# A recommendation tower on one core: warm-up transposes, single-table rounds first, and gathers tied to the pair products

## The reference, cut to what matters

```python
e = jnp.stack([tbl_0[ids[:, 0]], ..., tbl_25[ids[:, 25]]], axis=1)      # (512, 26, 128)
all_vecs = jnp.concatenate([dense[:, None, :], e], axis=1)              # (512, 27, 128)
interactions = jnp.einsum('bnd,bmd->bnm', all_vecs, all_vecs)
z = jnp.concatenate([dense, interactions[:, rows, cols]], axis=1)       # rows < cols
h = jnp.concatenate([z, dense], axis=1)
h = jnp.maximum(h @ W_top1 + b_top1, 0.0)                               # 607 -> 512
h = jnp.maximum(h @ W_top2 + b_top2, 0.0)                               # 512 -> 256
y = h @ W_top3                                                          # 256 -> 1
```

## Time and profile before

| | |
|---|---|
| median of 3 runs | 140.96 us (140.27 to 141.63) |
| the profiled execution: its own time | 141.28 us |
| the profiled execution: span from first to last instruction | 139.5 us |
| mean granted clock of TensorE, share of full | 0.902 |
| PE, PEld busy | 108.0 us (77%), 83.7 us (60%) |
| DVE, ACT, POOL busy | 82.8 us (59%), 51.2 us (37%), 70.7 us (51%) |
| moved from memory | 16.27 MB |

### The profile page before, as it was taken

How to read it: one execution, slowest core, us unless ns; L and a number is a source line. 1 busy time by engine, 2 the same in 40 slices (tenths; PEclk the granted TensorE clock), 3 DMA queues, 4 the chain that set the end, 5 groups by cost and what they waited for, 6 DMA issues and landing times.

```text
span 139.5 us, 3355 instructions
## 1 busy us (share of the span) xinstructions
PE 108.0 (77%) x1416; PEld 83.7 (60%) x1416; DVE 82.8 (59%) x173; ACT 51.2 (37%) x86; POOL 70.7 (51%) x60
## 2 busy tenths in 40 slices
PE   0079299999999999989985422279999995995971
PEld 0057188778888888867743311267588684683560
DVE  5286396999999999979989100055035266014101
ACT  3040561794949678089160000012042131040130
POOL 4787788888888888888888777200000000000000
PEclk9999959999999999999997555555799999999999
DMA  2999999999999999981111112100000000000000
GB/s 65 236 281 239 303 237 262 234 244 240 239 247 236 285 275 220 230 260 50 38 38 42 51 44 56 38 7 5 0 5 5 5 5 0 0 5 5 0 0 3
DMA packets 7677, 16.49 MB, mean 118 GB/s; under 512 B 2007, under 2 KB 2648, under 8 KB 7662
## 3 DMA queue, kind: packets, MB, share of 16 engines
q1 hardware_dynamic: 5998, 12.87, 37.6%
q0 software_dynamic: 1664, 3.41, 9.9%
HBM read 16.27 MB, written 0.00 MB: 117 GB/s over the span
## 4 chain that ended last, share of the span: by engine, by line
PE 40%; DVE 23%; issue 16%; DMA 12%; ACT 4%; SPq 1%; another core or an unknown queue 1%; POOL 0%; DVEq 0%; POOLq 0%
DVE hot L422 14%; DMA tab_raw<-in_tbl 12%; PE gram_ps L543 12%; DVE tab_lo L426 6%; PE fill_ps L595 6%; PE l_ps L566 4%; PE fill_ps L507 3%; PE fill_ps L509 3%; ACT vec L233 2%; PE l_ps L569 2%; PE l_ps L573 2%; PE fill_ps L529 2%; PE l_ps L570 2%; PE turn_ps L581 2%; DVE vec L412 2%
## 5 line engine op out<-in xcount | busy, mean ns | idle before, releaser
L327 POOL DMA_INDIRECT gathered<-in_tbl,ids_sb x52 | 69.8, 1343 | 16.6 <-issue 14.9
L507 PE MATMUL fill_ps<-hot,tab_hi 125*128 125x512 f32 x112 | 47.1, 420 | 8.8 <-issue 8.3
L509 PE MATMUL fill_ps<-hot,tab_lo 125*128 125x512 f32 x112 | 45.9, 410 | 0.0
L422 DVE TENSOR_SCALAR hot<-ids_bc,row_id 125x1024 fp32r<-125x1024 int32 (+1 forms) x60 | 42.8, 714 | 3.3 <-DMA ids_bc<-in_ids_t 2.1
L507 PEld LDWEIGHTS fill_ps<-hot,tab_hi 125*128 125x128 f32 x112 | 22.6, 202 | 14.9 <-issue 9.0
L543 PE MATMUL gram_ps<-vec 128*32 128x27 f32 x1024 | 17.5, 208 | 13.8 <-issue 13.8
L344 ACT CAST tab_hi<-tab_raw 125x512 fp32r<-125x512 f32 (+1 forms) x30 | 17.9, 610 | 25.8 <-DMA tab_raw<-in_tbl 16.6
L426 DVE TENSOR_TENSOR tab_lo<-tab_raw,tab_hi 125x256 fp32r<-125x256 f32 (+1 forms) x60 | 24.0, 400 | 5.4 <-issue 4.4
L543 PEld LDWEIGHTS gram_ps<-vec 128*32 128x32 f32 x1024 | 14.3, 123 | 18.8 <-issue 18.8
L509 PEld LDWEIGHTS fill_ps<-hot,tab_lo 125*128 125x128 f32 x112 | 22.5, 201 | 4.4
L459 DVE COPY_PREDICATED pairs<-second,gram_ps 128x104 f32<-128x104 int32 x16 | 4.4, 274 | 31.3 <-ACT pairs L383 31.1
(11 more groups left out here) (46 smaller groups left out, 61.5 us busy)
## 6 DMA issues: line engine op xcount, KB each, us to landing
tab_raw<-in_tbl SPq DMA_DIRECT2D x8, 448.0 KB
ids_bc<-in_ids_t SPq DMA_DIRECT2D x13, 256.0 KB
tab_raw<-in_tbl SPq DMA_DIRECT2D x4, 560.0 KB
gathered<-in_tbl,ids_sb POOLq DMA_INDIRECT x52
w_raw<-in_w_pairs SPq DMA_DIRECT2D x3, 256.0 KB
w_sb<-in_W_top SPq DMA_DIRECT2D x1, 512.0 KB
tab_raw<-in_tbl SPq DMA_DIRECT2D x2, 224.0 KB
tab_raw<-in_tbl SPq DMA_DIRECT2D x8, 52.0 KB
```

The lines of the kernel that those rows point to most:

```text
L327: pool.indirect_dma_start(out=gathered[:, n % GSLOTS, j, :], out_offset=None, in_=tables[f], in_offset=bass.IndirectOffsetOnAxis(ap=ids_sb ...
L422: nc.vector.tensor_scalar(hot[0:HP, (PIECE * c + k) % HOTS, 0:n, :], ids_bc[0:HP, slot, 0:n, :], row_id[0:HP, j:j + 1], None, ALU.is_equal ...
L507: nc.tensor.matmul(into, tab_hi[0:HP, c % PSLOTS, f, k * D:(k + 1) * D], one_hot, start=first, stop=False)
L509: used = nc.tensor.matmul(into, tab_lo[0:HP, c % PSLOTS, f, k * D:(k + 1) * D], one_hot, start=False, stop=last)
```

## The change

- PE first does eleven transposes of the identity matrix into `turn_ps`, whose result nobody reads; its wait for the identity moves there from the dense step.
- The round of tables 3 and 6 is split, so that the first three rounds have one table each; there are eight rounds instead of seven. The order of the steps is rewritten: batches stand later by one or two places, and `batch(2, 2)` and `batch(2, 3)` come after the first units of tile 1.
- SP loads the dense vectors behind round 2; the first half of table 2 is loaded from ACT's queue instead of SP's.
- Nine of the last sixteen gathers wait for a count of `gram_made`, two for a count of `l1_made`. POOL works in order, so those behind them wait too.
- `fill_copy` of a batch walks the same elements in another order: the n vectors of a sample, which lie side by side in `vec`, are now the innermost loop.

```diff
-ROUNDS = [[2], [3, 6], [7, 8], [19, 21], [23, 25], [0, 4], [5, 12]]
-NK = [8, 8, 8, 8, 8, 10, 10]
+ROUNDS = [[2], [3], [6], [7, 8], [19, 21], [23, 25], [0, 4], [5, 12]]
+NK = [8, 8, 8, 8, 8, 8, 10, 10]
+WARM_UPS = 11
-    out = hot(0) + [("dense",)] + hot(1) + batch(0, 0) + batch(0, 1) + hot(2) + batch(0, 2) + batch(0, 3)
-    out += hot(3) + batch(1, 0) + batch(1, 1) + hot(4) + batch(1, 2) + hot(5) + batch(1, 3) + batch(2, 0)
-    out += hot(6) + batch(2, 1) + batch(2, 2) + gram(0, 0, 1, 2, 3)
-    out += gram(1, 0) + batch(2, 3) + [("turn", 0)] + gram(1, 1) + [("l1", 0)] + gram(1, 2) + [("h1t", 0)]
-    out += gram(1, 3) + [("l2", 0)] + gram(2, 0) + [("turn", 1)] + batch(3, 0) + gram(2, 1)
+    out = hot(0) + hot(1) + batch(0, 0) + hot(2) + [("dense",)] + batch(0, 1) + hot(3) + batch(0, 2) + batch(0, 3)
+    out += hot(4) + batch(1, 0) + hot(5) + batch(1, 1) + batch(1, 2) + hot(6) + batch(1, 3) + batch(2, 0)
+    out += hot(7) + batch(2, 1) + gram(0, 0, 1, 2, 3)
+    out += gram(1, 0) + batch(2, 2) + [("turn", 0)] + gram(1, 1) + [("l1", 0)] + gram(1, 2) + [("h1t", 0)]
+    out += batch(2, 3) + gram(1, 3) + [("l2", 0)] + gram(2, 0) + [("turn", 1)] + batch(3, 0) + gram(2, 1)
+AFTER_GRAM = {(2, 3, 0): 1, (2, 3, 1): 2, (2, 3, 2): 4, (3, 0, 0): 5, (3, 0, 1): 6, (3, 1, 0): 7, (3, 1, 2): 8,
+              (3, 2, 1): 10, (3, 3, 1): 11}
+AFTER_L1 = {(3, 0, 3): 1, (3, 2, 2): 2}
...
-            return copy(vec[:, step[1], :, first:first + n].rearrange("p (g s) n -> p n g s", s=S),
-                        src[:, 0:n * P].rearrange("p (n s g) -> p n g s", n=n, s=S))
+            return copy(vec[:, step[1], :, first:first + n].rearrange("p (g s) n -> p g s n", s=S),
+                        src[:, 0:n * P].rearrange("p (n s g) -> p g s n", n=n, s=S))
...
             for t in range(TILES):
                 for i in range(NB):
...
                     for j, f in enumerate(BATCHES[i]):
+                        if (t, i, j) in AFTER_GRAM:
+                            pool.wait_ge(gram_made, AFTER_GRAM[t, i, j])
+                        if (t, i, j) in AFTER_L1:
+                            pool.wait_ge(l1_made, AFTER_L1[t, i, j])
                         pool.indirect_dma_start(
...
         @block.scalar
         def _(act):
+            half = NK[0] // 2 * D
+            for a, b in ((0, 112), (112, HP)):
+                act.dma_start(tab_raw[a:b, 0, 0, 0:half],
+                              tables[ONEHOT[0]].rearrange("(p k) d -> p (k d)", p=HP)[a:b, 0:half]) \
+                    .then_inc(first_half_landed, 16)
...
         @block.tensor
         def _(pe):
+            pe.wait_ge(ident_made, 1)
+            for _ in range(WARM_UPS):
+                nc.tensor.transpose(turn_ps[:, 0, :], ident[:], ident[:])
...
                     if kind == "dense":
-                        pe.wait_ge(ident_made, 1)
                         pe.wait_ge(dense_landed, 16)
```

More of the change, by code:

```diff
@@ L281, in load_tables @@
                     src = tables[f].rearrange("(p k) d -> p (k d)", p=HP)
-                    halves = [(0, NK[r] * D, table_landed[slot])]
-                    if r == 0:
-                        m = NK[0] // 2 * D
-                        halves = [(0, m, first_half_landed), (m, 2 * m, table_landed[slot])]
-                    for m, n, landed in halves:
-                        for a, b in ((0, 112), (112, HP)):
-                            sp.dma_start(tab_raw[a:b, slot, k, m:n], src[a:b, m:n]).then_inc(landed, 16)
-            sp.dma_start(ids_sb[:], ins["ids"].rearrange("(q t) f -> q t f", t=TILES)).then_inc(ids_landed, 16)
-            load_tables(0)
-            load_tables(1)
-            sp.dma_start(dense[:], ins["r_dense_proj"].rearrange("(q t) d -> q t d", t=TILES)) \
-                .then_inc(dense_landed, 16)
-            for r in range(2, NR):
+                    first = NK[0] // 2 * D if r == 0 else 0
+                    for a, b in ((0, 112), (112, HP)):
+                        sp.dma_start(tab_raw[a:b, slot, k, first:NK[r] * D], src[a:b, first:]) \
+                            .then_inc(table_landed[slot], 16)
+            sp.dma_start(ids_sb[:], ins["ids"].rearrange("(q t) f -> q t f", t=TILES)).then_inc(ids_landed, 16)
+            for r in range(NR):
                 load_tables(r)
+                if r == TSLOTS - 1:
+                    sp.dma_start(dense[:], ins["r_dense_proj"].rearrange("(q t) d -> q t d", t=TILES)) \
+                        .then_inc(dense_landed, 16)
                 if r == NR - 2:
```

## The result

The changed kernel took **148.26 us** (median of 4 runs, 147.17 to 148.96), the kernel before 140.62 us in the same job (4 runs, 140.07 to 141.63). The ratio is 1.053, with a 95% interval from 1.044 to 1.062: 5.3% slower, where 131.3 us were forecast. Some executions of any of these kernels are a few per cent slower than its others, and the ratios leave these out, so that they need not be the quotient of two medians. The profiled execution has a time of its own of 148.11 us, a span of 146.3 and a mean granted clock of 0.895.

The account below looks back on a forecast made before the run. It took the kernel's second half to be bound by PE's issue being throttled while POOL's gathers are in flight; -15.1 + 5.5 + 1.0 - 0.8 - 0.4 = -9.8 took 141.28 to 131.5, given as 131.3 us, range 124 to 140.

Parts of the forecast that it names:

- the first half: Stretch up to the last table's landing: single rounds and moved loads change nothing, 0 us, bounds -1.5 to +1.5.
- Rival E: Gathers one by one cost PE more than in a row, 2.5 us in each of eight units: 146 us; chance 0.09.
- Warm-ups: Eleven transposes at PE's start, 3.0 us, hidden while PE waits for ACT's first table data: cost 0.
- Last landing to unit 5: From the last table's landing through units 1 to 5: without gathers in flight unit 5 ends near 79.3, gain 15.1 us.
- Gathers put back: Sixteen gathers moved behind unit 1 hold up later units: +5.5 us, bounds 0 to 12.7.
- rival C: The gathers' throttle comes back whole in the later units, the full 12.7 us paid: 139.5 us; chance 0.13.
- Last landing +1.0: End of the gathers: the last ones land later and delay batch (3, 3), +1.0 us, bounds 0 and +1.5.
- Clock -0.8: Stretch 94 to 99 us and after: less time at half clock as PE is busier, -0.8 us, bounds 0 and -1.5.
- Copies: DVE's batch copies ahead of each tile's first unit get shorter by the new order: -0.4 us, bounds 0 and -0.7.
- rival B: All moved gathers hide, since only descriptor writing throttles PE and stock covers it: about 124.5 us; chance 0.15.
- rival D: PE's own instruction stream, not the gathers, stalls units 1 and 2, so the hole stays: 142.0 us; chance 0.07.

Follow-up runs that it names:

- r1: The kernel before, unchanged, run again in a later job for its own trace: 139.65 us (one run).
- r2: The changed kernel, unchanged, run again in a later job: 147.78 us against 138.73 for the kernel before, ratio 1.073.
- e3: The changed kernel with a wait on DVE's progress ahead of POOL's gathers 1 to 35: 139.84 us against 138.99 for the kernel before, ratio 0.997.
- r3: The kernel before with the round of tables 3 and 6 split, the order moved along and the dense load behind round 2: 146.84 us against 138.73.
- e1: The changed kernel with the old rounds, order and loads up to the last hot round, no warm-ups: 139.94 us, ratio 1.007 to the kernel before.
- r4: The changed kernel without the eleven warm-ups, where PE is held up: 148.40 us against 138.73 for the kernel before, ratio 1.078.
- e6: The changed kernel without the eleven warm-ups, in a job without the hold-up: 127.72 us against 126.55 for the kernel before.
- e4: The kernel before with four gates alone, letting ten gathers of tile 3 go in groups behind units that l1 or l2 follows: 134.10 us, ratio 0.942.
- e2: The kernel before with the 13 gathers of tile 3 left out, so tile 3's results differ from the reference: 128.65 us against 138.99.
- e7: The kernel before with four gates, at units 2, 6, 8 and 10, and the new copy order: 126.19 us against 126.55, ratio 0.995.
- t1: The kernel before with three small POOL memsets ahead of each of the last 13 gathers: 126.07 us against 128.08, ratio 0.984.
- s1: The changed kernel with three POOL memsets ahead of each of gathers 1 to 22: 141.27 us against 130.09 for the kernel before.
- e8: The kernel before with four gates, the new copy order and DVE's weight splits behind tile 0's last unit: 127.81 us, ratio 1.014.
- s4: The kernel before with four gates, new copy order and DVE's weight splits moved behind tile 0's last unit, run again: 128.08 us against 130.09.

## Why the prediction was wrong

**The step that failed: "I price the first half at 0, with bounds of -1.5 and +1.5".** It measured +8.4 (in job D, r1 to r2, +10.0). It rested on two sentences. One said that the transfers never pause; they paused for two slices. The other said that in the hot rounds "the same throttle would not show, since a matmul there lasts long enough". It shows there as late signals, not as gaps between products, and the late signal of 22.84 in the kernel before was a first trace of it. I had a hold-up by gathers and looked for it only inside the units. What kept it small in the front was, by the rows and e3, POOL's pace: in the kernel before, the twelve gathers beside round 0 and the wait behind it come 1.25 to 1.5 us apart, and those beside two-table rounds of DVE take 1.69 us each and come 2.0 apart. With one table in a round DVE's instructions are half as wide, POOL's take 0.94, and twenty of them come mostly 1.25 apart, until the slots are full. The price of a single round was asked of SP, DVE and PE, and never of POOL. That the split, with its order and dense load, is the trigger is shown (r3), and so is that slower gathers take the hole away (e3). Whether it is the rate as such, or the rate together with DVE's own stalls, is open.

**Rival E had the sign and the size (146) but not the way.** It put the loss into the tail, at 2.5 us for each of eight units. The tail costs about 1.2 on average, below its point of 1.9, and e1 shows that tail and gain cancel: 139.94. No rival had a loss ahead of the first unit.

**Warm-ups, 0: right.** They take 2.61 us instead of the 3.0 estimated, from 1.71 on; the first hot matmul comes at 6.14, behind 1.83 us of idle. Without them nothing changes (r4).

**Last landing to unit 5, -15.1: a little too large.** Units 1 and 2 passed as said. Unit 3 waited for DVE, as said, until 85.39. Units 3 to 5 then took 5.0 us instead of 2.3: three gaps of 1.0 us in sum, and a half clock (1.93 us for 115 products, window below). Two of the gaps lie beside the gather of 85.81; the third, at 89.36, beside that of 88.61 but also at the place of the gap that no gather explains (last section). Measured -12.4.

**Gathers put back, +5.5: too small, inside its bounds of 0 to 12.7.** Units 7, 8, 9, 11 and 12 with their neighbours pay 1.2 + 2.3 + 0.5 + 2.4 + 2.0 = 8.4 us, and units 3 to 5 about 1 more, inside the term above. The estimate that stock covers much of a unit was right for its first 41 to 46 products; behind them nothing passes but six in 0.75 us. The duration was wrong in the other direction: behind one or two gathers the hold-up lasts for the instruction and about 0.6 us, not until the landing. With 9.4 in all, rival C's "whole" (12.7) and the forecast (5.5) are about equally far off.

**Last landing +1.0: 0. Clock -0.8: wrong in its sign.** PE comes to the last batch at 122.81 and does not wait for it; its last gather was issued at 116.56. A batch that moved from ahead of unit 1 to behind unit 7 costs the tail 0.4, and the rest of the 10.8, about +2, lies mostly in stretches at half clock: the l2 at 118.85 took 2.89 us where 2.00 is usual, and l1's first pair took the same 2.08 us as before. In the windows of the kernel after (columns as in the earlier trace rows) both stretches lie near half clock:

```profile
120.00:123.50 3.50, 3.50 (x14) 2.80 (x12) 1.12 (x4) 0.44 (x1) 0.00 (x0) 0.54 0.01 2
```

```profile
85.30:90.40 5.10, 3.83 (x192) 3.21 (x192) 0.54 0.15 37
```

The second is of the pair products alone (columns as in the earlier trace rows). PE had stood in gaps through units 11 and 12 ahead of the first, and idle for 2.34 us ahead of the second. The clock gave nothing back.

**Copies, -0.4: the sign right, the copies shorter than estimated.** DVE's batch copy went from 808 to 564 ns, ACT's from 948 to 571. The rule that was set against this term (the Trainium skill, SBUF — State Buffer, the note on cachelines) would have given 0; whatever the PSUM side does with words 512 bytes apart, the trace shows that the sum of both is a gain of 244 and 377 ns. With one of DVE's copies on the path for each tile but the first that is an estimate of 0.7 us; no run has the copies alone.

**On a chip without the hold-up** nearly all of this is empty: the time before is 126 to 130, near rival B's number, there is no hole to close, and the change minus its warm-ups can't be told from before (e6). The forecast took one chip's weakness for the kernel's.

## What to carry to other kernels

When a step is split or moved, ask of every engine that runs beside it, POOL's queue too, at what pace it will now run, and whom that pace hurts; a queue that seemed free may have been held back by the very instructions that the change makes shorter. If short matmuls stand in gaps named "issue" beside indirect gathers, put the gathers in groups beside long matmuls (four gates, 5.8% in e4; gates alone were never run where nothing is held up, and gates with the new copies gave nothing clear there) instead of one into each gap of the schedule. And measure the kernel before on a second chip before trusting a hole of that kind, since the largest stall of this kernel, some 10 us, was absent in three of the six jobs.

## What was unexpected of the hardware

- **Gathers from POOL hold up PE on some chips.** Short products then pass in groups of five or six every 0.75 us, and PE's signals reach ACT and POOL 11 to 16 us late when twenty gathers follow each other at mostly 1.25 us. In jobs A, B and D this shows in every kernel with such gathers; in C, E and F in none. Before takes 138 to 141 us on the former and 126 to 130 on the latter. The front of before feels it a little on such chips (waits named "remote" of 2.1 us in before, 4.1 in r1), and in no trace of C, E and F does such a wait stand there. The way by which a gather's issue reaches PE's queue and signals is not known; whether PE's supply of instructions or its signals are held was not tested, nor whether the chip or something else of the job decides. The Trainium skill (SBUF — State Buffer, section "SBUF: two separate sides") says that only VectorE and GpSimd share a port and that PE never waits on anyone; a shared port of the two would fit POOL's 1.69 us beside wide DVE instructions against 0.94 beside narrow ones, though no run tells it from another cause. That PE never waits agrees with jobs C, E and F. In A, B and D it does wait; whether for a port is not shown.
- **The hold-up feeds itself.** Late signals stop DVE and ACT, an idle DVE leaves POOL at its quickest, and only full slots end it (POOL's last gather at 28.75, movement again within 5 us). This loop is an argument from the rows and from e3; no run broke it in another way.
- **A gap at fixed places of PE's own stream.** PE stands for 0.7 to 2.0 us when 306 products have passed, in e2 (1.62 us at 82.03, no gather in flight), e4, e6, e7, t1 and others, with and without the hold-up; the 1.04 us at 93.98 that rival D pointed at is the same place. In e3 and s1, which have the eleven warm-ups, it stands at product 295, which is 11 earlier. In e8 and s4 there is one more, of 1.46 and 1.55 us, at product 179, which is 127 before 306. So it belongs to a count of PE's instructions (127 products are 254 loads and matmuls), not to a gather, a wait or a time. What happens at such a place was not tested.
